# Routing weights gathered with the token rows, and a slot table that holds tokens alone

## What is computed

```python
x = x + tanh(g_ffn[l]) * ffn(layernorm(x))

# layer 0: E=8 experts, top K=2, width F=256, shared expert of width 1024
# layer 1: E=32 experts, top K=6, width F=192, shared expert of width 384
topk_w, topk_ids = top_k(scores(x @ w_gate), K)
topk_w = topk_w / sum(topk_w)
routed = sum over the K chosen experts e:  topk_w[e] * (silu(x @ g[e]) * (x @ u[e])) @ d[e]
shared = (silu(x @ sg) * (x @ su)) @ sd
ffn    = routed + shared
```

## Time and profile before

| | |
|---|---|
| median of 3 runs | 2045.34 us (2045.24 to 2046.21) |
| the profiled execution | 2046.07 us, of which the span is 2044.0 us |
| layer 0, shared half from g=1 | about 505 to 728 us |
| layer 0, experts | about 731 to 920 us |
| layer 1, FFN begins | about 1350 us |
| layer 1, shared half from g=1 | about 1408 to 1536 us |
| layer 1, experts | about 1538 to 2039 us |

### The profile page before, as it was taken

One profiled execution on the slowest core, in us unless ns is written; L12 is line 12 of the kernel. 1 busy time (PEld: TensorE's weight loads), 2 busy tenths in 40 slices (PEclk: granted clock), 3 DMA queues, 4 the chain that ended last, 5 costly groups with the idle time before them and its releaser, 6 DMA issues. The chain is left out here.

```text
span 2044.0 us, 40829 instructions
## 1 busy us (share of the span) xinstructions
PE 1886.2 (92%) x10024; PEld 1220.2 (60%) x10025; DVE 1348.0 (66%) x2556; ACT 1145.5 (56%) x1857; POOL 782.2 (38%) x941
## 2 busy tenths in 40 slices
PE   5999999989999999994999999987888999999998
PEld 2333333344888878872433333345667888888886
DVE  6899988841445544436889988859984555555553
ACT  1777777753322335541777777762224566666664
POOL 3222222125201125553222222127644656565555
PEclk9999999999999999995999999988999999999998
DMA  4422222142111458665422222131027888888886
GB/s 141 119 59 64 61 66 64 40 172 97 55 55 56 144 175 196 139 107 138 123 67 59 65 60 67 45 136 39 1 96 180 190 196 203 194 201 201 204 186 107
DMA packets 100082, 233.53 MB, mean 114 GB/s; under 512 B 17410, under 2 KB 20484, under 8 KB 99972
## 3 DMA queue, kind: packets, MB, share of 16 engines
q1 hardware_dynamic: 61572, 137.75, 23.7%
q0 software_dynamic: 33792, 79.71, 20.1%
q10 hardware_dynamic: 4608, 14.68, 2.2%
HBM read 127.23 MB, written 57.67 MB: 90 GB/s over the span
## 5 line engine op out<-in xcount | busy, mean ns | idle before, releaser
L599 DVE TENSOR_REDUCE maxima<-ring_ps 128x1 f32<-128x512 f32 x1024 | 639.8, 681 | 89.2 <-PE ring_ps L386 88.2
L493 ACT ACTIVATE probs<-score_ps 128x1024 f32<-128x1024 f32 x512 | 501.8, 1019 | 91.6 <-PE score_ps L403 89.3
L386 PE MATMUL ring_ps<-k_turned,q_turned 64*128 64x512 f32 x1024 | 414.3, 481 | 39.7 <-DMA q_turned<-q_lo 18.4
L386 PEld LDWEIGHTS ring_ps<-k_turned,q_turned 64*128 64x128 f32 x1024 | 179.0, 193 | 367.1 <-DVE maxima L599 258.0
L1179 PE MATMUL bank_f<-w_gu_parts_f,xg_T_f 128*128 x1800 | 367.1, 352 | 2.1 <-issue 2.1
L1179 PEld LDWEIGHTS bank_f<-w_gu_parts_f,xg_T_f 128*128 128x128 f32 x1800 | 325.8, 190 | 30.4 <-issue 3.0
L403 PE MATMUL score_ps<-q_turned,k_turned 64*128 64x512 f32 x1024 | 336.3, 447 | 1.7 <-ACT probs L493 1.4
L420 PE MATMUL out_ps<-probs,v_ones 128*32 128x512 f32 x2048 | 273.3, 606 | 10.7 <-issue 10.4
L1204 PE MATMUL bank_f<-w_dn_parts_f,hg_T_f 96*128 (+1 forms) x888 | 243.6, 410 | 1.5 <-DVE hg_T_f L1773 1.5
L983 POOL DMA_INDIRECT xg_f<-xh_rows_f,idx_in_f x156 | 159.5, 1022 | 186.1 <-DVE idx_in_f L1663 106.7
L999 POOL DMA_INDIRECT out_x<-y_tok_f,idx_out_f x111 | 177.2, 1596 | 133.0 <-ACT y_tok_f L1407 94.6
(11 more groups left out here) (232 smaller groups left out, 2335.2 us busy)
## 6 DMA issues: line engine op xcount, KB each, us to landing
w_gu_f<-in_L_w_gu SPq DMA_DIRECT2D x64, 384.0 KB
q_turned<-q_hi SPq DMA_DIRECT2D x128, 128.0 KB, 2.6
w_raw_f<-in_L_w_sh_gu ACTq DMA_DIRECT2D x28, 512.0 KB, 3.5
w_dn_f<-in_L_w_dn SPq DMA_DIRECT2D x32, 384.0 KB
k_turned<-k_hi SPq DMA_DIRECT2D x128, 64.0 KB, 2.1
q_turned<-no_max SPq DMA_DIRECT2D x64, 128.0 KB, 2.6
q_turned<-q_lo SPq DMA_DIRECT2D x64, 128.0 KB, 2.7
w_gu_f<-in_L_w_gu SPq DMA_DIRECT2D x16, 512.0 KB
```

The lines of the kernel that those rows point to most:

```text
L386: pe.matmul(ring(k, "max", i), q_turned[rows, slot, h // 2, c * P:(c + 1) * P], k_turned[rows, slot, :], start=True, stop=True).then_inc(m ...
L493: act.activation(probs[:, (TPB * u + c) % PROBS, pair, :, :], score_ps[:, pair, :, :], ACT.Exp, scale=float(D) ** -0.5).then_inc(exped, 1)
L599: dve.tensor_reduce(maxima[:, par, col:col + 1], ring(k, "max", i), AX.X, ALU.max).then_inc(max_taken, 1)
```

## The change

The routing weights (all `E` columns, `weight`) are stored in DRAM behind the normalised rows, which become `H + E` wide (2080 B in layer 0, 2176 B in layer 1), and come with the gather into `xg`. In the expert half ScalarE loads the tile's expert into a register after `x_hi`, and copies that column of `xg` into `table_sb[:, i, 1]`; the gather into a buffer also waits for that copy (`weight_taken`). The table carries the token alone: `weights_of` and `entry` are gone, `tile_hot` is 128 wide and made by `tensor_scalar` in place of `scalar_tensor_tensor`, the sum's matmul has 128 columns, and `finish_table` has two instructions less. VectorE makes the first `HOTS` tile one-hots right after the first `shared_w_lo`, in both layers.

```diff
-        xh_rows = dram("xh_rows", (ROWS, H))
+        xh_rows = dram("xh_rows", (ROWS, H + E))
...
-                sp.dma_start(xh_rows[b * S:(b + 1) * S, :].rearrange("(n p) d -> p n d", p=P), xh(b)
+                sp.dma_start(xh_rows[b * S:(b + 1) * S, 0:H].rearrange("(n p) d -> p n d", p=P), xh(b)
...
             sp.dma_start(w_sd_raw[:], t["w_sh_down"].rearrange("(c p) h -> p c h", p=P)).then_inc(down_in, 16)
+            sp.wait_ge(weight_made, 1)
+            sp.dma_start(xh_rows[0:TOK, H:H + E].rearrange("(n p) e -> p n e", p=P), weight[:]).then_inc(weight_stored, 16)
...
             pool.wait_ge(table_ready, 1)
+            pool.wait_ge(weight_stored, 16)
...
                 pool.wait_ge(xg_turned, i + 3)
+                pool.wait_ge(weight_taken, i + 3)
                 gather(i + 4, half)
...
-                mm = pe.matmul(bank[:, TABLE_BANK, 0:3 * P], slot_hot[:, n % HOTS, :],
-                               tile_hot[:, n % HOTS, :, :].rearrange("p c t -> p (c t)"),
+                mm = pe.matmul(bank[:, TABLE_BANK, 0:P], slot_hot[:, n % HOTS, :],
+                               tile_hot[:, n % HOTS, :],
...
                 act.activation(xg_T[:, half, 0, :, :].rearrange("p d m -> p (d m)"), bank[:, 6, :], ACT.Copy).then_inc(xg_hi, 1)
+                expert = act.value_load(sched[0:1, bass.ds(i, 1), 0:1].rearrange("a i c -> a (i c)"), min_val=0, max_val=E - 1)
+                act.activation(table_sb[:, bass.ds(i, 1), 1:2].rearrange("p a c -> p (a c)"),
+                               xg[:, half, bass.ds(expert + H, 1)], ACT.Copy).then_inc(weight_taken, 1)
...
-            then(dve.tensor_copy(entry[:, :, :, 0], token_f[:, :, None].to_broadcast([P, TT, K])))
-            def weights_of(first):
...
-                then(dve.tensor_tensor(chosen[:], row1[:, :, None, :].to_broadcast(shape),
-                                       top_rows[:, :, ks, None].to_broadcast(shape), ALU.is_equal))
-                then(dve.tensor_tensor(chosen[:], chosen[:], weight[:, :, None, :].to_broadcast(shape), ALU.mult))
-                then(dve.tensor_reduce(entry_w[:], chosen[:], AX.X, ALU.add))
-                then(dve.tensor_copy(entry[:, :, ks, 1], entry_w[:]))
-                then(dve.tensor_tensor(entry[:, :, ks, 2], entry_w[:], entry[:, :, ks, 1].bitcast(F32), ALU.subtract))
...
-                dve.scalar_tensor_tensor(tile_hot[:, n % HOTS, :, :], count_f[:, None, :].to_broadcast([P, 3, P]),
-                                         tile_of[:, i, k:k + 1],
-                                         entry[:, i, k, :, None].bitcast(F32).to_broadcast([P, 3, P]),
-                                         ALU.is_equal, ALU.mult).then_inc(tile_hot_made, 1)
+                dve.tensor_scalar(tile_hot[:, n % HOTS, :], count_f[:], tile_of[:, i, k:k + 1], token_f[:, i:i + 1],
+                                  ALU.is_equal, ALU.mult).then_inc(tile_hot_made, 1)
...
-                then(dve.tensor_copy(table_sb[:, 0:P, 1], bank[:, TABLE_BANK, P:2 * P]))
-                dve.tensor_tensor(table_sb[:, 0:P, 1], table_sb[:, 0:P, 1], bank[:, TABLE_BANK, 2 * P:3 * P], ALU.add
-                                  ).then_inc(table_ready, 1)
...
-            weights_of(0)
             shared_x_lo(1)
             shared_w_lo(FC, 0)
             shared_w_lo(FC, 1)
-            for k in range(KS, K, KS):
-                tile_one_hots(HOTS)
-                weights_of(k)
+            tile_one_hots(HOTS)
```

More of the change, by code:

```diff
@@ L696, in make_ffn @@
             if layer == 0:
-                tile_hot = first_use.enter_context(nc.sbuf_tensor(f"tile_hot_f{layer}", [P, HOTS, 3, P], F32R))
+                tile_hot = first_use.enter_context(nc.sbuf_tensor(f"tile_hot_f{layer}", [P, HOTS, P], F32R))
         w_gu = sb("w_gu", [P, 2, HC, 2 * F])
         w_dn = sb("w_dn", [FW, 2, FK, H])
-        zero_tile = sb("zero_tile", [P, H])
+        zero_tile = sb("zero_tile", [P, H + E])
         table_sb = sb("table_sb", [P, SCHED, 2])
-        with ExitStack() as last_use:
-            chosen = last_use.enter_context(nc.sbuf_tensor(f"chosen_f{layer}", [P, TT, KS, E], F32))
         above, tied, tmp, prob, weight, mask, row1 = (sb(n, [P, TT, E]) for n in
@@ L731, in make_ffn @@
             xh_fourth = first_use.enter_context(nc.sbuf_tensor(f"xh_fourth_f{layer}", [P, TPB, H], F32))
-        xg, y_tok = sb("xg", [P, 2, H]), sb("y_tok", [P, 2, H])
+        xg, y_tok = sb("xg", [P, 2, H + E]), sb("y_tok", [P, 2, H])
         if layer == 1:
@@ L748, in make_ffn @@
             if layer == 1:
-                tile_hot = sb_first("tile_hot", [P, HOTS, 3, P], F32R)
+                tile_hot = sb_first("tile_hot", [P, HOTS, P], F32R)
         w_gu_parts = sb("w_gu_parts", [P, 2, 2, HC, 2 * F], F32R)
@@ L776, in make_ffn @@
         gate_done = sem("gate_done")
+        weight_made, weight_stored, weight_taken = sem("weight_made"), sem("weight_stored"), sem("weight_taken")
         h_made, hs_hi, sd_hi, sd_split = sem("h_made"), sem("hs_hi"), sem("sd_hi"), sem("sd_split")
@@ L786, in y0 @@
         def y0(c):
-            return (y_tok if c < 2 else xg)[:, c % 2, :]
+            return (y_tok if c < 2 else xg)[:, c % 2, 0:H]
         def raw_w(n, o):
@@ L1015, in _ @@
                 pool.wait_ge(xg_turned, i - 1)
+                pool.wait_ge(weight_taken, i - 1)
                 gather(i, i % 2)
@@ L1521, in _ @@
             then(dve.tensor_scalar(stat2[:], stat2[:], gate[:, 0:1], None, ALU.mult))
-            then(dve.tensor_tensor(weight[:], prob[:], over_e(stat2), ALU.mult))
+            dve.tensor_tensor(weight[:], prob[:], over_e(stat2), ALU.mult).then_inc(weight_made, 1)
             dve.wait_ge(ranked, 1)
@@ L1680, in finish_table @@
                                               ALU.is_lt, ALU.mult))
-                then(dve.scalar_tensor_tensor(table_sb[:, 0:P, 0], bank[:, TABLE_BANK, 0:P], -1.0, part, ALU.add, ALU.add))
-                then(dve.tensor_copy(table_sb[:, 0:P, 1], bank[:, TABLE_BANK, P:2 * P]))
-                dve.tensor_tensor(table_sb[:, 0:P, 1], table_sb[:, 0:P, 1], bank[:, TABLE_BANK, 2 * P:3 * P], ALU.add
-                                  ).then_inc(table_ready, 1)
+                dve.scalar_tensor_tensor(table_sb[:, 0:P, 0], bank[:, TABLE_BANK, 0:P], -1.0, part, ALU.add, ALU.add
+                                         ).then_inc(table_ready, 1)
                 dve.wait_ge(table_ready, 1)
```

8 lines of the change are left out of this document (2 added, 6 removed).

## The result

| | before | after |
|---|---|---|
| median of 5 runs each, us | 2046.21 (2045.24 to 2048.28) | 2028.75 (2026.00 to 2034.70) |
| ratio, with its 95% interval | | 0.9923 [0.9911, 0.9936] |
| the profiled execution, us | 2046.07 | 2032.16 (span 2030.5) |

What follows compares the result with a forecast made beforehand. TensorE, busy 92% of the span, bounds the kernel, waiting for late VectorE in layer 1's shared half. -14.5 - 4.8 - 2.6 - 1.6 + 3 = -20.5 us from 2046.1: 2025 us median, range 2010 to 2042.

Steps and rivals of the forecast that it cites:

- g=1 of layer 1: Layer 1's shared half: VectorE's lateness goes, gate and up take 23.1 us in place of 37.6, saving 14.5 us.
- TensorE should run through: Layer 1, g=1: eighth slot one-hot at 1411.5, wanted at 1413.2, so TensorE makes 36 sums without waiting, 23.1 us.
- Narrow matmul: The sums' matmul, 384 to 128 columns: taken as 0; bounds -8 us (-6 in layer 1) and +6 us.
- It leaves 0.17 us to the next start: Start-to-start time of the 384-column sum matmul, kept for the 128-column one, so 0 saved.
- the 1.6 of the vanished wait: Layer 1, g=2: TensorE's single wait for a tile one-hot goes, saving 1.6 us.
- Steps between groups and clock: Layer 1, g=1 to 2 and 2 to 3: earlier additions save 4.8 us, less half clock 2.6 us (bounds 0, 5.2).
- Experts: Both layers' expert halves: ScalarE's load and copy, later gathers and wider rows cost +3 us; bounds 0 and +0.35 a tile.
- So 0.7 to 0.8 us against 0.99: Expert tiles: ScalarE's new load and copy, 0.7 to 0.8 us, fit into its 0.99 us a tile of waiting for TensorE.
- the point of 0.16: Expert tiles: from 0.16 us lost a tile on, the kernel is slower than before and the prediction falls.
- the third rival: Experts, chance 0.13: ScalarE's waiting doesn't cover the work, or the gather's ring becomes longest; 2059 us at 0.25 a tile.
- The ports: Layer 1's shared half, rival, chance 0.10: narrow one-hots lock GpSimd out, a pair takes 0.80 us; 2031 us.
- Layer 0 and the rows' bytes: Layer 0's weights_of gives 0, its shared half stays within 2 us; 2176 B rows add 6% to the gathers.

Runs made afterwards that it cites:

- load_early: The kernel after, with layer 1's register load of the expert moved ahead of x_hi's wait for the transposes; ratio to before 0.9906, layer 1's experts 505.7 us.
- copy_no_wait: The kernel after, but layer 1's ScalarE copy reads a fixed tile of weights and gathers don't wait for it; ratio to before 0.9912, experts 514.6 us.
- vector_copy: The kernel after, but VectorE, not ScalarE, does the register load and weight copy, right behind an index copy; ratio to before 0.9937, experts 518.5 us.

## Why the prediction was right, and where it wasn't

**g=1 of layer 1: the number right, by two errors that cancel.** Said 23.1 us from the last down matmul of g=0 to the first of g=1 (-14.5); measured 23.4 (1409.4 to 1432.8, -14.2). That VectorE's lateness would go, and TensorE no longer wait for it, was right. But "TensorE should run through" was not. 36 sums at the 0.574 us of g=2 are 20.7 us; the other 2.7 us are waits for GpSimd, which set the pace from the eighth sum on, and which the narrow matmul's 36 x 0.066 = 2.4 us, counted as 0, happened to cover. The eighth slot one-hot came at 1413.2, not 1411.5, so nothing was in hand any more. And a slot one-hot lasts 0.60 us beside VectorE's narrow one-hots but longer beside its lo parts: 0.98 us at 1413.74, 1.05 at 1421.50, 1.49 at 1425.50. The sum at 1427.04, 1.36 us behind the one before it, is what that last one cost. A tile one-hot takes 0.34 us and not 0.2, which cost nothing here.

**Narrow matmul: mis-sized.** Taken as 0; it is worth -0.066 us a sum, about the lower bound of -0.06 that the transposes gave. In layer 1 that is 3.7 us and not 96 x 0.066 = 6.3, because GpSimd took g=1's part back, as the bounds had allowed. "It leaves 0.17 us to the next start" was the wrong row to stay with: the next matmul starts after 0.06 us and then takes 0.28 in place of 0.23, behind a weight load of 0.19 us that a 128-column matmul doesn't cover. The g=2 stretch fell by 4.5 us, 2.4 of it the narrow matmul, where I had only the 1.6 of the vanished wait; g=3's fell by 1.5, where I had nothing.

**Steps between groups and clock: too much.** Said -4.8 and -2.6; the two down stretches with them lost 2.7 and 2.8 us, 5.4 in all. The wait is 2.4 us, not 1.8, because the one-hots take 2.0 us and not 1.4; and after it 18 matmuls still took 6.0 us against 4.1 at full clock. The granted clock of the two stretches in the earlier trace rows rose from 0.86 and 0.90 only to 0.96 and 0.95: a wait of 2.4 us was still followed by matmuls at half clock, so most of the clock's part didn't come. It isn't the same in every execution: in `load_early` the same wait of 2.37 us was followed by 18 matmuls in 4.75 us, and the down stretch of g=1 takes 13.0 to 13.1 us in six of the kernels above, and 14.25 in after. What decides that isn't shown.

**Experts: the step that failed.** "So 0.7 to 0.8 us against 0.99: it fits, less well where an expert changes." 0.99 us was a mean over tiles of two kinds. In the tiles where the expert changes ScalarE had 0.16 us of it (the earlier trace rows has 71 and 58 waits in 107 tiles), and there the load's 0.8 us came on top of a tile that was already longer than TensorE's. +11.2 us in layer 1 is 0.10 us a tile: within the bound I gave (0 to 0.35) and short of the point of 0.16 where the kernel would have become slower; it is the mild form of the third rival. `copy_no_wait` shows that of its two mechanisms ScalarE's own time is the cause, and the gather's wait for the copy is not; the gathers are late all the same, behind the scatter that waits for `y_out`.

**The ports: the rival fell, but not the effect behind it.** Narrow one-hots don't lock GpSimd out: a pair takes 0.57 us in g=2, and up to two tile one-hots lie beside one slot one-hot, which stays at 0.60 us. (The rival's +1 for g=2 was a slip besides: 29 x 0.80 = 23.2 against 23.1.) The Trainium skill ("SBUF — State Buffer", two separate sides) has the shared pair of ports held for the whole instruction if VectorE's has two SBUF inputs or runs in a two-port mode. If the tile one-hot were of that kind, 0.34 and 0.60 us as measured would make 0.94 us a pair; this trace has 0.57, so for this pair of forms it doesn't come out. For VectorE's `TENSOR_TENSOR` on two SBUF tensors it does. The slot one-hot that starts at 1402.20 lasts 2.90 us beside lo parts that end at 1404.11 and 1404.71, and all 17 slot one-hots over 0.7 us in after's layer 1 lie beside such an instruction. It holds the other way too: VectorE's one-hots at 1410.70 and 1411.94 last 1.33 and 1.32 us, each as long as the GpSimd addition beside it (1.28 and 1.27).

**Layer 0 and the rows' bytes: right.** Nothing to see of `weights_of` there, nothing of 2176 for 2048 B. Layer 0's shared half is 1.2 us longer, inside the 2 us I had allowed, for the unexplained rate of its matmuls.

From one profiled execution to the other the forecast was -20.5 us and the measured difference in span -13.6. The shared half of layer 1 gave 3.4 us more (26.9 for 23.5), the experts of both layers cost 6.5 more, and layer 0's shared half and the rest 1.2 and 2.7. That the median came out only 3.75 us from the forecast is in part luck: after's profiled execution was 3.4 us slower than its median, and before's was at it.

## What to carry to other kernels

An engine's idle time per tile, taken as a mean, says nothing about whether new work fits: split the tiles by kind, and look at the one in which that engine has no waits. When work must be moved to another engine, ask what stands behind it in that engine's order, not how busy the engine is. A wait for a DMA can be a late engine two queues earlier; only a run that takes the nearest suspect away (here the gather's wait) tells. And a number that comes out is no proof of its terms: g=1's did, with TensorE held by GpSimd, which shows at TensorE's weight loads and not in its list of waits.

## What the runs showed of the hardware

- A register load on ScalarE lasts 0.28 us, but with its register work it put the copy 0.80 us behind the start of `x_hi` (1592.18 to 1592.98, its first register instruction stands at 1592.18 too). On VectorE in `vector_copy` the copy waited 0.87 us in the mean. The Trainium skill ("DMA: Bandwidth & Descriptors", latency and other measured facts) gives some 600 ns as the floor of a `tensor_load`, without saying from where it loads; the trace has less for the load itself, and more for all that stands with it.
- Behind a 128-column fp32r matmul the next one starts after 0.06 us (0.17 behind a 384-column one), and the one after that comes 0.05 us later than otherwise: a third of the columns saved 0.066 of 0.64 us.
- VectorE's `TENSOR_TENSOR` on two SBUF tensors and a GpSimd instruction beside it keep each other out for the whole instruction (2.90 us for a 0.60 us slot one-hot, 1.33 us for a 0.34 us tile one-hot beside GpSimd's addition). VectorE's 128-column `TENSOR_SCALAR` and GpSimd's run side by side at 0.34 and 0.60 us.
- fp32r matmuls of 512 columns came 0.227 us apart in layer 0's g=1 of the three kernels built on before and 0.233 in the eleven built on after, in the same code at the full granted clock; the cause is open.
